# Layer 1 opens in another order: batch 0's maxima first, batch 1's norm and projections between and behind them

## What is computed

```
qkv = x @ W_qkv.T + b_qkv                      # 16 heads of 16
scores = einsum('bnqd,bnkd->bnqk', q, k) * scale
attn = softmax(where(causal, -inf, scores))    # 512 x 512 per head
out = einsum('bnqk,bnkd->bnqd', attn, v)
x = layernorm(x + out @ W_out.T + b_out)
```

## Time and profile before

| | us |
|---|---|
| median of 3 runs | 929.6 (929.55 to 932.98) |
| the profiled execution | 930.34 |
| its span, first to last instruction | 928.2 |
| TensorE busy | 815.7 (88%) |
| VectorE busy | 455.8 (49%) |
| ScalarE busy | 376.9 (41%) |

### The profile page before, as it was taken

One profiled execution on the slowest core, in us unless ns is written; L12 is line 12 of the kernel. 1 busy time (PEld: TensorE's weight loads), 2 busy tenths in 40 slices (PEclk: granted clock), 3 DMA queues, 4 the chain that ended last, 5 costly groups with the idle time before them and its releaser, 6 DMA issues. The chain is left out here.

```text
span 928.2 us, 12127 instructions
## 1 busy us (share of the span) xinstructions
PE 815.7 (88%) x4099; PEld 439.0 (47%) x4100; DVE 455.8 (49%) x1321; ACT 376.9 (41%) x597; POOL 97.5 (11%) x111
## 2 busy tenths in 40 slices
PE   5498999999998989999997687978999979979986
PEld 3222434444435556666654334434454535533675
DVE  2722652563425712222245794777754764553263
ACT  3287775784761101111133113545332433156130
POOL 0000000000000011111631101231011101011000
PEclk9689999999999999999989698989899989999999
DMA  6467317016034151111114680004500180000000
GB/s 199 95 177 133 122 43 144 12 30 122 1 108 143 32 164 46 45 45 45 34 59 133 185 258 16 2 24 121 153 1 2 51 245 1 2 1 24 12 12 24
DMA packets 54848, 71.12 MB, mean 77 GB/s; under 512 B 8182, under 2 KB 49178, under 8 KB 53258
## 3 DMA queue, kind: packets, MB, share of 16 engines
q1 hardware_dynamic: 52924, 65.33, 25.9%
q0 software_dynamic: 1872, 5.11, 2.1%
HBM read 46.57 MB, written 23.72 MB: 76 GB/s over the span
## 5 line engine op out<-in xcount | busy, mean ns | idle before, releaser
L610 PE MATMUL ps<-arena 128*128 128x256 f32 (+5 forms) x1084 | 336.9, 460 | 17.7 <-DVE arena L1203 5.0
L610 PEld LDWEIGHTS ps<-arena 128*128 128x128 f32 (+1 forms) x1084 | 204.8, 199 | 108.4 <-issue 69.5
L931 ACT ACTIVATE arena<-ps 128x1024 f32<-128x1024 f32 x128 | 124.1, 1026 | 39.8 <-PE ps L644 39.6
L1369 DVE TENSOR_REDUCE arena<-ps 128x1 f32<-128x512 f32 (+3 forms) x176 | 101.2, 634 | 42.5 <-PE ps L834 41.7
L1023 ACT ACTIVATE arena<-ps 128x1024 f32<-128x1024 f32 (+3 forms) x128 | 83.2, 705 | 87.4 <-PE ps L856 87.2
L602 PE MATMUL ps<-arena 128*128 128x128 f32 (+4 forms) x429 | 68.6, 304 | 44.3 <-DVE arena L1090 17.7
L723 PE MATMUL ps<-arena 128*128 x184 | 88.0, 602 | 1.2 <-DVE arena L1274 1.2
L602 PEld LDWEIGHTS ps<-arena 128*128 128x128 f32 (+4 forms) x429 | 54.4, 154 | 66.2 <-DVE arena L1090 21.3
L644 PE MATMUL ps<-arena 96*128 96x512 bf16 x256 | 71.5, 392 | 12.4 <-DMA arena<-parts_dram 9.3
L832 PE MATMUL ps<-arena 96*128 96x128 bf16 (+3 forms) x256 | 65.0, 312 | 12.5 <-DVE arena L1369 6.7
L1458 POOL TENSOR_SCALAR_AFFINE_SELECT arena<-arena 128x512 f32<-128x512 f32 x64 | 42.2, 661 | 288.7 <-ACT arena L1023 288.5
(11 more groups left out here) (142 smaller groups left out, 701.5 us busy)
## 6 DMA issues: line engine op xcount, KB each, us to landing
arena<-stacks_dram SPq DMA_DIRECT2D x16, 768.0 KB, 6.4
arena<-in_gate_up_proj SPq DMA_DIRECT2D x8, 1024.0 KB, 9.7
arena<-parts_dram SPq DMA_DIRECT2D x48, 128.0 KB, 4.5
stacks_dram<-arena SPq DMA_DIRECT2D x16, 384.0 KB, 3.4
arena<-in_down_proj SPq DMA_DIRECT2D x8, 512.0 KB, 9.1
stacks_dram<-arena SPq DMA_DIRECT2D x16, 256.0 KB, 3.7
parts_dram<-arena SPq DMA_DIRECT2D x8, 384.0 KB, 4.3
yg_dram<-arena SPq DMA_DIRECT2D x23, 128.0 KB, 1.7
```

What stands on the lines that cost most here:

```text
L610: last = nc.tensor.matmul(dst[0:rows, lo:hi], a, w, start=(n == 0), stop=(n == len(pairs) - 1))
L931: nc.scalar.activation(probs[:, 2 * p:2 * p + 2, :], ps[:, 2 * p:2 * p + 2, :], ACT.Exp)\
L1369: nc.vector.tensor_reduce(mneg[:, qt, h0:h0 + nh], filled(v, step)[:, 0:nh * w].rearrange("p (h n) -> p h n", n=w), AX.X, ALU.max, negate= ...
```

## The change

Only `C_START` and `C_FIRST` are different. The same steps are done, with the same operands.

```diff
 C_START = """Wb0 Wat0 Wat1 Wat2 Wu0 Wul0 Wu1 Wul1 Wu2 Wul2 Wu3 Wul3 cL0 Wq0 Wq1 Wq2 Wo0 Wd0 Wd1 cX0 cL1 Wd2 Wd3 cX1 cQ0 cQ1 cK0 cQ2
-cK1 cQ3 cK2 cV0 cK3 cV1 Wdl0 Wdl1 +cL0 Wdl2 +cX0 +cL1 Wdl3 +cX1 m +cQ0 m +cK0 m m +cQ1 m m m m +cK1 m m
...
+cK1 cQ3 cK2 cV0 cK3 cV1 m m m m m m Wdl0 m m Wdl1 m m Wdl2
...
++cK1 +cQ2 | +cQ3 +cK2 | +cV0 +cK3 | +cV1 | +m +m +m +m | +m +m +m +m | +m +m +m +m | +m +m +m +m |
```

More of the change, by code:

```diff
@@ L82 @@
 C_START = """Wb0 Wat0 Wat1 Wat2 Wu0 Wul0 Wu1 Wul1 Wu2 Wul2 Wu3 Wul3 cL0 Wq0 Wq1 Wq2 Wo0 Wd0 Wd1 cX0 cL1 Wd2 Wd3 cX1 cQ0 cQ1 cK0 cQ2
-cK1 cQ3 cK2 cV0 cK3 cV1 Wdl0 Wdl1 +cL0 Wdl2 +cX0 +cL1 Wdl3 +cX1 m +cQ0 m +cK0 m m +cQ1 m m m m +cK1 m m
-+cQ2 m m m +cK2 m m +cQ3 m m m m +cK3 m m m m m m m m m m m m m m m m m m m m +cV0 m m m m m cM0 +cV1"""
-C_FIRST = """+m | | +m +m | +m | +m +m | +m +m +m +m | +m +m +m | +m +m +m +m +m | +m +m +m +m | +m +m +m | +m +m | +m
-+m +m +m +m | +m +m +m | +m +m +m +m +m +m +m +m +m | +cM0 >cL0 | >cL1 |"""
+cK1 cQ3 cK2 cV0 cK3 cV1 m m m m m m Wdl0 m m Wdl1 m m Wdl2
+m m Wdl3 m m m m m m m m m m +cL0 m m m m m m +cX0 +cL1 m m m m m m +cX1 m m +cQ0 m m
++cK0 m m +cQ1 m m m m cM0"""
+C_FIRST = """+cK1 +cQ2 | +cQ3 +cK2 | +cV0 +cK3 | +cV1 | +m +m +m +m | +m +m +m +m | +m +m +m +m | +m +m +m +m |
++m +m +m +m | +m +m +m +m | +m +m +m +m +m | +m +m +m +m +m | +m +m +m +m +m | +m +m +m +m +m | +cM0 >cL0 | >cL1 |"""
 C_SECOND = """-cF0 -cF1 +cX0 | -cG0 -cF2 -cF3 +cX1 +cQ0 | -cG1 +cK0 -cP0 +cQ1 | -cP1 +cK1 +cQ2 | +cQ3 +cK2 =cO0 +cK3 |
```

## The result

The changed kernel takes 935.8 us (median of 5, 932.1 to 937.9) where the kernel before takes 929.6 (5 runs, 929.0 to 933.0). The ratio is 1.0075, with a 95% interval of 1.0054 to 1.0097: slower by 0.75%, 6.2 us. A second set of runs of the same two kernels gave 935.2 and 928.8, 1.0067 (1.0044 to 1.0090). The ratios leave out four executions of the later sets that took 999 to 2011 us. The forecast was 930.3 and no change, with a range up to 935.3. A slowdown clear of the noise was not forecast, and the time lies just outside the range.

A forecast was written before the change was run, and what follows sets the result against it. VectorE was taken to bind in batch 0's maxima, TensorE in the attention slots. Five terms put batch 1's last reduction at 610.0 against 609.29, 0.7 us later: median 930.3, no change, range 925.3 to 935.3.

The forecast's parts named there:

- Term 1: Start of batch 0's maxima: the first maximum at 514.1 in place of 525.25, 11.1 us earlier.
- Term 2: Stage of batch 0's maxima: its work and pauses end at 557.6, before 565.3; 7.7 us gained up to here.
- My other sum: Same stage reckoned from its old length of 39.0 us: now 43.3 us, ending at 558.5 at the latest.
- Term 3: M0 to the first scores: the chain keeps its 4.45 us, M0 isn't held up, scores start at 562.1.
- Term 4: First scores to batch 1's first reduction: 19.2 us, with four projections open in the slots and 2.3 for the clock.
- Term 5: Batch 1's 44 maxima in ten attention slots: 28.8 us, bounds 27 and 30.5, last reduction at 610.0.
- even filling: Batch 1's maxima: slots with three left VectorE idle 0.4 to 0.9 us each; evenly filled slots give some back.
- The slower one: Rival: clock stays at 1.2 GHz through slots 0 to 3, +5.4 us, median 935.7; chance 0.18.
- The late stack: Rival: batch 1's second stack lands too late for maximum 22; 2 us late gives 932; chance 0.05 with the rest.
- the change did what it says: Opposite of a rival: stack lands later than 514.1, so the head start shrinks; given almost nothing.
- The faster rival: Rival: 3.2 us of pauses among batch 0's maxima, projections at 2.4 GHz, 44 maxima in 27.3; median 925.2; chance 0.17.

The follow-up runs named there:

- the opening alone: Kernel before, slots kept: Wdl products first, then batch 0's maxima with batch 1's norm, Q and K steps among them, K1.3 sixteen maxima ahead of M0; 931.3 us.
- The first form of the opening alone: The opening alone, but with K1.3 only six maxima and V1.0 ahead of M0, against the kernel before; 936.8 us (1.0080).
- V1.1 back: Changed kernel with V1.1 moved from slot 3 to between M0 and the first scores; 938.1 us, 933.3 in the one execution of its second profile.
- the Wdl edit: Changed kernel with the four Wdl products again ahead of the first maximum, all else as in it; 931.1 us (1.0038).
- the slots alone: Kernel with the old order of the opening and the attention slots of the changed kernel; 927.8 us (0.9988 to the kernel before).

## Why the prediction was wrong, step by step

**Term 1 was right in size.** The first reduction came 7.3 us behind the second load, as forecast.

**Term 2 failed, by 3.3 us (45.7 against 42.4), and it is the largest miss.** Of this 2.5 us are pauses: the sum had 4.1, and the trace has 3.62 + 0.77 + 2.26 = 6.65. I took 1.0 us for the Wdl products. The pauses there were 0.48 + 0.42 + 1.36 + 1.36 = 3.6. I had the price of one product at the slow clock, 2.04 us, and its cover, 1.7, in the text, and still reckoned as if each product stood alone. The two maxima behind it in TensorE's order also have to be computed before VectorE can go on, and at 1.2 GHz TensorE can't keep up: from 520 to 528 us it was busy 7.99 of 8 us and VectorE 5.27. From one product's start to the next it took 522.99 − 520.01 = 2.98 us, for which VectorE has one addition and two reductions, 0.61 + 1.01 = 1.62. The difference is the pause of 1.36. The pause at the transposes was 0.8 where I had 0.4, those at Q1.0 and Q1.1 were 2.3 and 0 where I had up to 3.4 in all. Putting the products back alone returned 5.2 us, moving them alone cost 2.2.

The other 0.8 us is work. I counted the 44 reductions as 24.3 us, but in VectorE's timeline of the kernel before they take 25.3 (0.69 + 0.69 + 3.51 + 2.74 + 3.58 + 10.97 + 3.08). My other sum, 43.3 us from the length of the old stage, had this right, and I took the lower one.

The first stage offered little to begin with. TensorE waited from 514 to 525, but VectorE was busy 15.4 of 16.6 us there: it did the norm then, and in the new order it does it later. That the opening alone leaves M1 at 101.6 against 101.5 shows that nothing was won by it. My sum did have this in it, since the 9.7 and 2.5 us stood beside the 11.1, but the small difference of large terms hid the question of how long VectorE would be idle.

**Term 3 was right,** 4.5 us, and that K1.1's stores behind the moves don't hold M0 up. The first form of the opening alone shows what it costs to have two loads close ahead of them, 5 us.

**Term 4 was right in size, 18.6 against 19.2,** and Q1.2 took 3.62 us where I had charged 3.46. Its explanation was half right. I put the slow clock to V1.1's removal. With V1.1 back, Q1.2 took 1.88 us in one profile and 3.62 in two. The prediction cites for this a rule of the Trainium skill, "TensorE: Matmul & The Clock Gate", section "Why this matters for your kernels"; the traces agree with it where V1.1 took 3.78 us (three profiles, with 1.88 for the projection behind it) and not where it took 2.76 or 2.88 (two, with 3.62). In the median the removal cost less than the 2.3 us that I charged: V1.1 back on top of the Wdl edit changed 931.1 to 931.1.

**Term 5 was 1.0 us too small,** 29.8 against 28.8. The step that failed in it is the saving by even filling, about 1.6 us in my sum (28.0 + 2.4 − 28.8). Between the first reduction and the last, VectorE's pauses in the ten slots sum to 4.7 us against 5.2 for forty maxima before, so it saved 0.5. The four more maxima cost 2.3, near the 2.4 reckoned, and the bound of 30.5 held.

**From the stretch to the median** 1.5 us are left over: the profiles have 4.7, the medians 6.2 and 6.4. Behind M1 the changed kernel's two profiles take 313.1 us from the first exponentials of batch 1 to the end, the one before 313.5, so no profile shows them. The two profiles of the changed kernel are of short executions with a higher clock than the others, and the first profile with V1.1 back, whose instructions up to M0 are the same, lost 2.9 us more to the clock. That the median execution loses more in the same place is likely, but not shown. The other experiments too have medians that lie 0 to 5 us further above the kernel before than their stretches say.

**The rivals.** The slower one named a time that is nearly the measured one, 935.7 against 935.8, but that is chance, for its mechanism was another: it had the clock low through slots 0 to 3, and its test was a granted clock under 0.7 in the 15 us behind the first scores. It was 0.74 (last section), and Q1.3, V1.0 and V1.1 took 1.88, 1.95 and 1.89 us, and the slots alone made the kernel no slower. The late stack didn't come, and the change did what it says. The faster rival needed a stage with 3.2 us of pauses, which had 6.65, and Q1.2 at 2.4 GHz.

## What to carry to other kernels

Where the work of a stretch is only put in another order, first find the engine whose work must be done before the stretch can end, and count how long it stands idle in the old order and in the new; another engine's wait is worth nothing while that one is working. Where a step is inserted between short producer steps, compare one round of the producer with one of the consumer: once the results that stand ready are used up, each round costs the difference, here 2.98 − 1.62 = 1.36 us. Reckon it at both clocks, since such a step took 1.1 us at one and 2.04 at the other. And small transfers that gate a stage should not have large loads close ahead of them on the same queue.

## What the runs showed of the hardware that I had not expected

TensorE was busy 7.99 of 8.00 us from 520 to 528 us in the changed kernel and stayed at a granted clock of 0.50, 1.2 GHz, all through. It ran products with 16 rows, score products with 96 rows and mask products with 128 rows in that time. Later, in the slots, it was at 2.4 GHz with less to do:

```profile
562.90:577.90 15.00, 14.64 (x60) 5.64 (x61) 3.13 (x6) 7.88 (x13) 2.55 (x4) 0.74 0.72 201
577.90:611.30 33.40, 31.25 (x269) 15.29 (x267) 28.31 (x51) 16.45 (x26) 7.01 (x11) 1.00 0.27 72
```

The first profile with V1.1 back shows it more strongly: 18.00 of 18.00 us busy, from 516 to 534, at 0.50. In its second profile, with the same instructions, two of the four pauses at the additions were shorter, since the clock was up for a while. So a TensorE that is busy by the profile's count doesn't always bring the clock up, and the order of instructions alone doesn't decide it. What does, no run here separates.

A second observation stays without a cause. In three of thirteen profiles there was a longer pause ahead of batch 2's first projection, and the clock fell behind it. From batch 1's first exponentials to the second head group's took 20.7 to 21.5 us in these, and 17.6 to 18.8 in the others. ScalarE's first row below, from the kernel with the Wdl products first, is an evacuation that begins 1.3 us after its transposes ended (at 619.8); the second is the projection's:

```profile
621.08 0.60 ACT L1000 ACTIVATE arena<-ps 128x512 f32<-128x512 f32 x1 [2.04 <-PE ps L602]
624.78 1.26 ACT L1013 ACTIVATE arena<-ps,arena 128x512 f32<-128x512 f32 x2 [3.10 <-PE ps L610]
```

Such pauses are worth 3 us, as much as several of the edits here. In the profile with the Wdl products first this is 3.1 of the 3.8 us by which the program behind the changed stretch took longer than before. With one profile for a kernel, the distances inside the changed stretch are the best measure, and they too moved by 2.9 us between two profiles of one kernel. The losses of 5.2 and 5.8 us in the opening stand clear of that; differences of 1 to 3 us between single profiles do not, unless the pauses themselves are shown.
